# Other step orders for the five engines of a fused two-layer transformer kernel

## The reference, cut to what matters

```python
xn = _layernorm(x)
x = x + _L0_attn_ref(xn, ...) + _L0_ffn_ref(xn, ...)
xn = _layernorm(x)
x = x + _L1_attn_ref(xn, ...) + _L1_ffn_ref(xn, ...)
return x
```

## Time and profile before

| | us |
|---|---|
| three timed runs | 1861.48, 1868.83, 1850.03; median 1861.48 |
| the profiled execution | 1868.28 |
| its span, first to last instruction | 1866.3 |
| PE busy in the span | 1686.1 |
| DVE busy | 1315.3 |
| ACT busy | 960.0 |
| POOL busy | 826.7 |

### The profile page before, as it was taken

The page is one execution under the profiler, slowest core; times in us unless marked ns, Lnnn a source line. Parts: engine busy times, 40 slices in busy tenths (PEclk is TensorE's granted clock), DMA queues, the critical chain, the costliest instruction groups (busy, mean ns, idle before and its releaser), DMA issues. The chain is left out here.

```text
span 1866.3 us, 44130 instructions
## 1 busy us (share of the span) xinstructions
PE 1686.1 (90%) x16808; PEld 1117.8 (60%) x16808; DVE 1315.3 (70%) x3530; ACT 960.0 (51%) x2513; POOL 826.7 (44%) x827
## 2 busy tenths in 40 slices
PE   6697799998999999899999989999999999998787
PEld 3564477565765667566675657656675566755443
DVE  4754596877768777777777778777777778776383
ACT  4335444575345744476445854367434764456333
POOL 5509462554426543453525635265334544363000
PEclk9888899999899999999999999999989999999797
DMA  7310312103210032101222033101221013200020
GB/s 246 69 30 12 80 44 79 32 10 89 78 53 19 22 80 70 55 19 39 66 75 59 5 83 84 54 21 36 49 83 53 19 36 100 79 22 5 15 78 7
DMA packets 160002, 100.56 MB, mean 54 GB/s; under 512 B 59160, under 2 KB 147352, under 8 KB 159512
## 3 DMA queue, kind: packets, MB, share of 16 engines
q1 hardware_dynamic: 159504, 96.94, 19.5%
q10 hardware_dynamic: 288, 0.81, 0.2%
HBM read 55.36 MB, written 27.28 MB: 44 GB/s over the span
## 5 line engine op out<-in xcount | busy, mean ns | idle before, releaser
L1337 ACT ACTIVATE shared<-bank 128x512 f32<-128x512 f32 (+1 forms) x384 | 202.0, 532 | 207.4 <-PE bank L1044 205.1
L1825 POOL TENSOR_TENSOR soft<-soft,prec 128x512 f32<-128x512 f32 x128 | 132.3, 1040 | 372.6 <-DVE prec L1470 372.1
L1634 DVE TENSOR_REDUCE nmx<-bank 128x1 f32<-128x512 f32 (+3 forms) x352 | 222.8, 637 | 92.6 <-PE bank L1016 90.8
L1237 ACT ACTIVATE soft<-bank,nmax 128x128 f32<-128x128 f32 x512 | 180.2, 380 | 102.5 <-DVE nmax L1462 101.6
L1787 POOL TENSOR_TENSOR qk_rs<-qk_rs,minus_half 128x16 f32<-128x16 f32 x64 | 187.6, 2931 | 5.3
L1044 PE MATMUL bank<-shared 75*128 75x384 bf16 (+3 forms) x512 | 141.7, 305 | 0.0
L695 PE MATMUL bank<-w_sb,hT 128*128 128x512 f32 x256 | 136.6, 624 | 5.5 <-DVE rot L1452 3.1
L1043 PE MATMUL bank<-b_sb 128*128 128x128 bf16 x512 | 114.6, 225 | 25.7 <-ACT shared L1337 22.5
L1016 PE MATMUL bank<-shared 72*128 72x256 bf16 (+3 forms) x512 | 126.5, 299 | 0.0
L1043 PEld LDWEIGHTS bank<-b_sb 128*128 128x128 bf16 x512 | 49.1, 99 | 115.9 <-ACT shared L1337 70.1
L663 PE MATMUL bank<-c_sb,soft 128*128 128x128 f32 x608 | 96.7, 290 | 22.9 <-POOL soft L1825 17.7
(11 more groups left out here) (254 smaller groups left out, 4479.7 us busy)
## 6 DMA issues: line engine op xcount, KB each, us to landing
shared<-parts_dram SPq DMA_DIRECT2D x64, 288.0 KB
vm<-v_f SPq DMA_DIRECT2D x112, 128.0 KB, 2.4
parts_dram<-parts SPq DMA_DIRECT2D x96, 128.0 KB, 2.4
L_dram<-the SPq DMA_DIRECT2D x32, 256.0 KB, 2.4
shared<-Z_dram SPq DMA_DIRECT2D x32, 256.0 KB, 3.3
shared<-L_dram SPq DMA_DIRECT2D x32, 256.0 KB, 4.1
shared<-X_dram SPq DMA_DIRECT2D x32, 256.0 KB, 4.9
w_sb<-weights SPq DMA_DIRECT2D x1, 4167.0 KB, 17.8
```

The source lines that it names most:

```text
L1237: a = af(v4(p_sb, 2, 4)[:, j, g], place("fS", j)[:, g * P:(g + 1) * P], ACT.Exp, bias=nmax[:, at:at + 1], accum_out=psums[:, at:at + 1])
L1337: af(v4(PTm, 2, GROUP)[:, u % 2, i, 0:n], place("mST", b, i)[:, 0:n], ACT.Exp).then_inc(mexp_done, 1)
L1634: reduce(v3(nmx[:], HM)[:, h:h + len(heads), c], v3(place("mS", b, t)[:, 0:len(heads) * (c + 1) * P], len(heads)), AX, ALU.max, negate=Tru ...
L1825: tt(p, p, spread(prec[:, at:at + NPAIR], P), ALU.mult).then_inc(fnorm_done, 1)
```

## The change

The five strings of `ORDER` are replaced by five others of the same lengths and with the same number of each letter. Nothing else in the file differs: the streams, the steps, their instructions and waits, the tiles and banks are the same. Of PE's 22 lines the first four are shown, of SP's all two; ACT's, DVE's and POOL's strings change in the same manner.

```diff
--- before.py
+++ after.py
@@ -39,67 +39,67 @@
 ORDER = {
     "PE": (
-     "fefefededffefdddefeeeeffebefefbbbbfffbffbbfbfbfddddbfddfddbbddbddddbddbdddedbdbddbdbdbddddbdbbddbbddddbbdbddddff"
-     "dddffffffffbdebbebefbeffbffdfebbbebeffebeeedbbebffebfbdbbffdbbbdffbbbbbbbbddffffbdbmffdmbbdbmfbffbddmfddmbdbmddb"
-     "ddbmfdmdffdddbdmdmffdbbddbddbddmdbddmddddbbdbdbdmbdddmdedbmdbbmbbabbabamafaafmdfafafamafmaffambamfcafamcbabcfacb"
-     "ccabcmafcmacfaccabcamcaffbcabcfccabcamcbaceccaecaffcaeacbaffcacebcabecabcabacbccafcaefabcaecabeccabaecbcaecabcca"
...
+     "fefefedefffdddeeedeefeffebeebffbbbfffffbbbbffbfddddbdffdddbbddddbdddbdbdddddbdbdbdbdbddddbdbbbbddddddbbdbeddddff"
+     "dddffffffffbdebebbefffebbfedffbbbeefbfebeeedbbebffebfbdfbbdbfbbffdbbbbbbbbffddfffbbdmdmfbbdbmffbfbddmfddmbbdmddb"
+     "dbdfmddffmdddbddmffmdbbddbddbdmddbddmddbddbdbdbdmdbddmddbdmbmbbbeabbabamafamafaffaamfdamfaffambamfacfamcabbcfcab"
+     "cacbcmfacmacfacacbcamfafcabccfccababcmacbcecceacfacfaeacbaccffaeabcbacebacbacbccafaecafbecbacaeccabacebcaecabcca"
...
     "SP": (
-     "fffeeeeeeeddffddffeffeeeeeddfemfdffdmaffaaffaaeeeeeeeddffcddmffmaffaaffaafeeeeeeeddmfcmffddaafffafaaeeeeeffedded"
-     "dmmffaffcafaafaefeeeeeeddffmmcfddaffaaffaaeeffeeeeeddddfmcfmaafffaafafeeeeeeddddcffmmfaafffafaacmmaaaaac"),
+     "feeefeeeeffddddffffeeefeeedfdefffddmmaaffafafeaeeeeeefddmfffmddcafaffaafeaeeeefeefddmcffddmaffafafaeaeeeeeedfdfm"
+     "mdcffdaafffafaeeaeeeeeddcffmmffddaaffaffafeeeafeeeddemmddffafcaffafaeaeefeeefdddmdffmacafffafaammacaaaac"),
 }
```

More of the change, by code:

```diff
@@ L47 @@
[L47 to L51, removed]
@@ new lines @@
+     "ccbcmacbcaeccaeacffaecabcfacacefacbbeacbacbacbccaecaffabcaecabeaccbaecbceabcfaccecfcfacecbfbbbbccbbcecbcffcccfcc"
+     "bccccfccdcbcdcdmdmdbmbfbdfbfdddbddfmddmfbbddmbdddfdbdmdmfdfdbddffmdmebbmdddbdddbddbddmdddddbbdbmbdddbdmddbdmbmbb"
+     "bbababamafamaffadfafmaamafffambmafacfamcbbacfacbaccabcmafcmcafccabcacmaffbcabcfaccbcamacbceccaecafcfaeacbcacffea"
+     "bcabeacbcabacbccaacffeacbbaceaeccabcaebacecabcaecffecfccbceccbbfbbcbbccfccbcfcfcfcccccbcdcmfcbcddmddbbmbdbfddfdb"
+     "ddffmddmbbddbddmdbdmdfdmffdddbdmdfmbfdbdbdddbddmdbddmdddedbbbdbddmdddbmddmdbmbbbbabbabamafaaffamfaamfaafmdfafmba"
@@ new lines @@
+     "cccaccaacaacacacaccaacccaccaacccaacccaaccacaccaaccacccaccccccccccccccccccccccccc"),
+    "ACT": (
+     "ffefefeedffdeedfeeefffbbffbbfffffbbbdbdfffbbbbffdddbdbdbdbbbdbddeffdddffffffbdefbbefbefefffbfebbbfeeffeebbbbffff"
+     "bdddbbbffbbddffffffbfbbbmfbfmffbbbbffmmdmmfmddfdbfddbbbfmbbbbdbdddmddbebmfffffdmfffbcfcbcbfcmbfccccffccbfcccbfmc"
+     "bbcfcceccecffecbcecbbfcbfcfccebecfecfcbbcebcecbccccffcccfbcfcccfccffccfccccbdcbdddbbmdfbfffmbbbbmfmmmfdffddmbddd"
+     "fbbbmfbbbbdbddmdddebbmffffdfmfffbcffcbcbcmbcccfcffccbfccfcbbmccbccfecefcfeccbcefcbbcbcffcecbcebcefcbefcbcebcccfc"
+     "cfccfbcccfcfcfcccccfccbfccddbdddmbbbfffmfbbbmbffdmmmffdmddbffbdbdmbbbbbdbddmdeddbbmfffffmdfffbfccmbbccbfcfccfcfc"
+     "cbfccmbbcccfbccfeccecffecbcecbbecffbcfccbccefecfbbcebcecbccffccfcccbcccffccfcccccfcfcbcdbdddmbbdbmfffbbbffbmdmmm"
+     "fdffdmdbbddbfbfmbbbbdbddmdeddbbmffffffmdffbfccbfcbcmbcccfcffccbcfcmfcbbcbcccfeccefcfecbcebccbffcbfeccbcecefcfbbe"
+     "cbcecbccccfccfcbcccffcccccccccffdcbddbffddbbmmbfffbffbbbmmmmdfddfmfdbfddbmfbbbbbbdbdddmddebbmfffffdmfffbcfcbcfbm"
+     "cbfccccffccbfcfmcbbccbccfcecefcfcecbcecbbcebffcfccbcecfecbebfcbcebccccffcccffbccccfcfccfccfccccbddcbdddbmbffbmff"
+     "bbbbmmmmffddmdffbfddbbfdbmbbbbdbddmdddbebmffffdfmfffbfccmfcbbcfbccccffccbcfmccbbfcbcccfeccecffcebcecbbefcbcfcfcb"
+     "cececffbbecbcecbcccffccfccbccccfccffccccccdfddfdcdbbmbbfbmfffdfddbdddbbfbmffmmmbbmbdfbdfdbddbbmdbbmbmbfdfcccfcff"
+     "ccffcfmfccbccfcbbbfmfcffcbccfcmcbbccfcbffccccbcbbfcbfcccbccbbcbcbccccccbccccccccccbcccmmmmmmmmmmmmcccccccccccccc"
+     "cmcccccccccccccccccccccccccccccccccccccc"),
@@ new lines @@
+    "DVE": (
+     "ffffeeeeeffeebebbeffbebfbbfeddddbdbdbdbddddddddbdbddbbeddbbddbddbdbddddddbddbbbddddffffdbbbffeeeebbfbbfbbeebbeee"
+     "bbfbbebbfbbbbbbffdbddbfbmbdbfmemmdbdmmmbddmbbfdmddmdddfdbmmdmddmbbmbddddmddbmddbdbdbdddmddebbdmbddbmbmmbadbbdaba"
+     "amafafamafamafmaambamababfaafammaaabmababafbaaamfmcaabaaaeebababaaeeababaabbaacafaafbbaabaeebefecbefbbbebbfcfbbe"
+     "cbmmdmdddmmmbmddbmdbbddmdddfddmdmfmdbmddmbmbbmddeddbddddmbdbddbmddddbbdmbddmbbddmbabbmabaamafafamafamafamambamab"
+     "bafaafamambaamabababfafmacambaaaeeaababeabeaaababacbabaaafafbbeaabebaefbaebfbbecbbecbfcbbmfmmdemddmbdmmdddbmbbdd"
+     "mddfmddmddfbdmmddbmebmbdmdddddbdmdbdbddddmbddmbbddbdbmbmmbbadbdabaamafafamafamafmaambamabbafaamafabmaamabababfaa"
+     "mamcfaaaeabeabbabaeeaaababaabcbaaaefafaabbeabaebfebfebbbcebbfcebcmbbmfdmmbddmmmddbddmbbddddmfddmddmfbmdmddmbmbeb"
+     "dmdddddbddmbddbddbdddbbmdmddbmbmbbababdmbadamafafaamafamafmambamabbafafamaamabmaabababfacmamaafabeaaabaebabeaeaa"
+     "babababaacaffaabbeaebaeabbfcebebfbebcbecbmbbmfdmfddbdmddbmmmbddmbdmfddmmddddfmdmmbddbmbbdmdmddeddbddbddbdbddmddb"
+     "bdmbddbmmbbabdbdmabaamafafamafamafamambamabbafaafambamaamabababfamcaamfbaaaaeeabababaeeaababacbabaafaafaebbaebaa"
+     "befbeefcbbbefbbcfbbbcmdmedmdmddmmmdbbddbmdbdmdmddfdmdbmfdmmdbdbmbddmdddddmbdbdbddbmddddbbedmbddbmbmddbabbmabaama"
+     "fafamafamafmaambaabbmafafmaabaamaambababfamcafamaaabaabebaebaeeaaabababeaabcaafafabbaeabaebfbebecbbfebcbffdcmdbd"
+     "bddbdmddmmdddbmmddmddfdfbddbmdbmdddmdbdddmddbdbdmddbdmmdbbddmbbmmmbbddamabamabambaaamabbabambamaaffaamffaamafbab"
+     "ambamfaabmaafbcmababmafaamaaababababaaamabacbaabbaaaabbbbbcbbbbbcmcmmmmmmmmmmmmmmmmmmmmmmaaaaamamaamamaamaamaaaa"
+     "aaaamaaaaaaaaaacaaaaaaaaaaaaacaaaammcmcc"),
@@ new lines @@
+    "POOL": (
+     "fffeeeeefffffbbffffffffbbfffeffbbbbbfffffdbfbfffffffebbeefffeeffbbffbbfbffffffbffffbbembbfffffffffbbbbbdfffffffb"
+     "bffffffbbfffffffbbeeebbeebffffffffffbbbfffmffbbeffffbbfbbbdffffffffbbffffbbffffffffbbeeeeebbbffffffbffffbbffmebb"
+     "ffffffffbbbbbdffffffffbbfffbbfffffffffbbeeeeebbbffffffffbefffbbmbbfffffffffbbbbbdffffffffbbfffffffbbfffffbbeeeee"
+     "bbfbffffffffbbbffffmbffbefffffbbbbbdfffffffbbfffffffbbffffffbbeeeeebbfbffffffffbfbbffemfffbbfffffbbbbbdfffffffff"
+     "fbbffffbbffffffbbeeeeebbbfffffffffbfbfbffffmbbfffffbbbbbdffffffffffbbfffbbfffffffbbbbbbm"),
```

58 lines of the change are left out of this document (12 added, 46 removed).

## The result

The changed kernel takes 1928.55 us (median of 4 runs, 1917.45 to 1935.67) against 1864.67 for the kernel before on the same chip (4 runs): a ratio of 1.0356, interval 1.0315 to 1.0397. It is 64 us slower. The prediction had the direction, but its 24 us are a good third of the loss, and 1928 lies outside its range.

What follows compares the result with a forecast made beforehand. It took PE, busy 1686.1 of 1866.3 us, as the bound, with its waits and clock. Terms 31 + 2 - 10 + 1 + 0 = +24 us on the median 1861.48 gave 1885 us; range for 8 in 10: 1836 to 1908.

Steps and rivals of the forecast that it cites:

- The neighbours: PE steps one place behind the PE step their operand hangs on, 76 to 127: the 51 new uncovered waits cost +31 us.
- the pairs behind mST: New mST-behind-mST and mPV-behind-mST neighbours on PE, 16 at 0.59 us each: 9.4 us.
- the nine of other kinds: Nine new uncovered PE neighbours of other kinds, priced at the mean 0.61 us each: 5.5 us.
- A third given back: While PE stands, ACT and DVE empty their queues and later waits shrink: -10 us, bounds nothing to all 31.
- the first three terms: PE's waits: uncovered neighbours +31 us, 24 more pairs at two places +2, part given back -10.
- SP, +1: In the start, SP issues four more transfers before the first inv_load, which PE's first inv_v needs: +1 us, bounds 0 and 2.4.
- The other moves of SP and POOL: SP's other moves, by one or two places in a mostly waiting queue, were taken as 0; POOL got no separate term.
- The clock: PE's clock level over the span: does not follow the order alone, so 0 us, bounds -29 to +15.
- no change: A PE wait at a new place is one less further on, nearly all 31 us given back: some 1865 us, chance 0.30.
- faster: New places keep PE busier and its clock higher: net -18 us, 1843, or 1820; chance 0.25 for under 1843.
- Rival 3: Slower by more: nothing given back, highest neighbour price, clock loses 15 us: +64, 1925 us; no own chance given.
- The signs: PE busy within 1% of 1686 us, idle up some 20; mST, mS, U_sb waits up; like stretches' mean clock 0.95 to 0.97.

Runs made afterwards that it cites:

- e1: Changed kernel with 48 pairs of adjacent PE steps swapped, uncovered neighbours 127 to 79: 1927.55 us, ratio 1.0344 to the kernel before.
- e2: Kernel before with 61 swaps in PE's order, uncovered neighbours 76 to 137: 1921.97 us, ratio 1.0343.
- e3: Kernel before with only SP's and POOL's orders of the changed kernel: 1907.36 us (median of three), ratio 1.0254.
- e5: Kernel before with the changed kernel's order on PE alone, save a few pairs: 2014.95 us, ratio 1.085.
- e6: Kernel before with the changed kernel's orders on DVE, ACT, POOL and SP, save a few pairs, PE as before: 2023.61 us, ratio 1.0903.
- e4: Changed kernel with eight unread matmuls added behind each of 24 mST steps at which PE next stops: 1905.99 us, ratio 1.0237 to the kernel before.
- e9: Changed kernel with the same eight matmuls behind 24 other mST steps after which PE does not stop: 1932.72 us, ratio 1.0389 to the kernel before.
- e10: e4 with 15 more fills at single stops in the same head groups of the changed kernel: 1906.26 us, ratio 1.0266 to the kernel before.
- e11: All five orders of the changed kernel up to step x1(3) (883 us), then those of the kernel before: 1901.42 us, ratio 1.0219.

## Why the prediction was right or wrong, step by step

- **The neighbours, +31 us:** right in kind as a sum of waits, somewhat small. The 51 more wait 45.2 us more (42.4 at the upper level), 0.89 each against the 0.61 that I had made of the timeline's rows; the largest misses are the pairs behind mST (14.3 us for 9.4) and the nine of other kinds (9.2 for 5.5). That the time hangs on them is not shown: e1 took 36 us of these waits away and the time stayed, and e2 may hold the price of its 61 swaps as such.
- **A third given back:** held, in one trace of each kernel. All other steps at the upper level waited 14.1 us less, a third of 42.4. The third was a guess, so that is luck. Net +28 us, where the first three terms gave +23.
- **SP, +1:** held in size. In the changed kernel the first inv_load is issued at 70.75 us, against 68.92 in the earlier trace rows, behind these:

```profile
68.25 0.52 SPq L1892 DMA_DIRECT2D vm<-v_f  x1
...
70.10 0.60 SPq L1894 DMA_DIRECT2D vm<-v_f  x1
70.75 0.59 SPq L1922 DMA_DIRECT2D shared<-Z_dram  x1
```

  PE's first inv_v begins 1.1 us later (77.57 for 76.47), of which x_tm's own later start is half.
- **The other moves of SP and POOL, 0:** open. e3 shows that these orders cost some 48 us (means) in a kernel whose DVE order they don't fit; what they cost in the one they do fit wasn't tried, and e5 and e6 say that a half can't show it.
- **The clock, 0, bounds -29 to +15:** this is the step that failed: a term set to nothing. It cost 27 to 38 us, outside its bounds, where the terms for waits together, +24, measured 29 to 40. The failing sentence is that "a PE that waits in many short pieces is still a PE that works in each of them". Clumps of such short waits bring the lower level on (e4 against e9, e10 against e11), and a lower stretch then costs up to half its length while PE is fully busy. These clumps carry about half of the 77 us that the changed kernel has more at the lower level; what brings on the other half is open. I had compared three like stages of one trace, saw 0.66 and 1.00, and took the clock for chance; one trace can't tell chance from run to run from the order's doing. The clock varies by run, 0.954 to 0.972 for one kernel, but its mean follows the order. The Trainium skill, "TensorE: Matmul & The Clock Gate", in its section on psum-queue depth-cycling, says that a PE which idles for very short times between groups of matmuls can make the clock swing between its levels; e4 with its control agrees (55 us less at the lower level), and I had not set this rule against my zero.
- **The rivals:** no change and faster fell. Rival 3 named 1925 us, by another sum: nothing given back (a third was) and 15 us for the clock (27 to 38).
- **The signs:** idle +20 (it was +25) and the waits for nmx (+7.4) came; U_sb rose by 0.8 only; mST's in this list not at all; PE's busy time rose by 1.8%, not within 1%, and the mean clock of 0.947 lay just under 0.95 to 0.97: the last is the clock speaking, and of PE's busy time most.

## What to carry to other kernels

When a new order makes PE stop more often in short clumps, price the clock along with the waits: here it cost about as much again. A few idle matmuls in the clumped stops recover part of that, and only there; place them by the trace and measure, since in the kernel before the same edit gained nothing that the runs can tell. Don't read a sum of waits as a sum of time to be won: covering 48 uncovered steps won nothing. And take orders of several engines over together: half of a fitted set lost more than twice what the whole set lost.

## What I had not expected of the hardware

The lower level outlasts the stops by far: 29.8 us at 0.50 with PE busy in 29.78 of them. 192 added matmuls made the kernel 22 us faster, and the same 192 placed elsewhere did not. And of the kernel's own spread over 27 runs (1850 to 1875 us) nearly all goes with the clock: a straight line of 0.35 us for each us at the lower level leaves at most 4.8 us either way.
